# A two-layer graph network: when GpSimd waits for PE before it gathers, and what is prepared first

## What is computed

```python
def _L0_gnn_ref(hn, src, dst):
    sums = jax.ops.segment_sum(hn[src], dst, num_segments=N_NODES)
    deg = jax.ops.segment_sum(jnp.ones((dst.shape[0],)), dst, num_segments=N_NODES)
    return jnp.where(deg[:, None] > 0, sums / jnp.maximum(deg[:, None], 1.0), 0.0)

def _L1_gnn_ref(features, abs_distances, rel_vec, edge_index, w1, b1, w2, b2):
    R = jax.nn.relu(abs_distances[:, None] @ w1 + b1) @ w2 + b2      # 384 radial weights per edge
    Y = spherical_harmonics(rel_vec)                                 # of rel_vec / |rel_vec|
    ...
            acc = acc + _NORM[i] * jnp.einsum('euv,ef,evi,ofi->euo', Rb[..., k], Yf, Fb, C)
    ...
    return out.at[dst].add(msg)

x = _layernorm(x + _L0_gnn_ref(x, src, dst), axis=-1)
x = _layernorm(x + _L1_gnn_ref(x, edge_weight, edge_attr_3, edge_index, ...), axis=-1)
```

## Time and profile before

| | us |
|---|---|
| median of 3 runs | 5155.01 |
| lowest and highest run | 5135.04 and 5165.75 |
| the profiled execution | 5126.5 |
| its span in the trace | 5124.8 |
| mean granted clock of PE in it | 0.879 |

### The profile page before, as it was taken

The page is one execution under the profiler, slowest core; times in us unless marked ns, Lnnn a source line. Parts: engine busy times, 40 slices in busy tenths (PEclk is TensorE's granted clock), DMA queues, the critical chain, the costliest instruction groups (busy, mean ns, idle before and its releaser), DMA issues. The chain is left out here.

```text
span 5124.8 us, 49999 instructions
## 1 busy us (share of the span) xinstructions
PE 3895.7 (76%) x15196; PEld 1997.9 (39%) x15196; DVE 3493.9 (68%) x4460; ACT 685.1 (13%) x1038; POOL 2969.8 (58%) x3001
## 2 busy tenths in 40 slices
PE   3777777777777777874388888888888888888862
PEld 1334343333333333332244444444444444444432
DVE  7655565555655555554478787878878888887864
ACT  0110101010101010100011111111111111111110
POOL 3555454555454545455566666666666666666645
PEclk9888888888888888886599999999999999999985
DMA  2101010010100101000122222222222222222211
GB/s 62 31 22 27 19 30 21 19 27 22 29 19 21 28 21 27 21 20 19 28 48 51 47 47 47 54 47 48 47 47 50 52 47 47 49 52 47 47 33 20
DMA packets 168166, 184.47 MB, mean 36 GB/s; under 512 B 57123, under 2 KB 135238, under 8 KB 161608
## 3 DMA queue, kind: packets, MB, share of 16 engines
q1 hardware_dynamic: 72486, 134.98, 9.3%
q0 software_dynamic: 95648, 49.16, 6.6%
HBM read 121.30 MB, written 62.61 MB: 36 GB/s over the span
## 5 line engine op out<-in xcount | busy, mean ns | idle before, releaser
L566 POOL DMA_INDIRECT got<-x_d,idx x1568 | 1601.8, 1022 | 818.4 <-issue 467.8
L834 PE MATMUL ps_r<-wc,hid 128*128 128x384 f32 x3136 | 1215.1, 529 | 378.4 <-DVE prod L1409 327.9
L834 PEld LDWEIGHTS ps_r<-wc,hid 128*128 128x128 f32 x3136 | 623.2, 205 | 981.5 <-DVE prod L1409 440.4
L762 PE MATMUL ps_r<-rest_f,hid 128*128 128x448 bf16 x1715 | 689.1, 402 | 216.0 <-DVE prod L1136 136.1
L1401 DVE TENSOR_TENSOR prod<-ps_r,f_along 128x768 f32<-128x768 f32 (+1 forms) x588 | 507.6, 863 | 425.2 <-PE ps_r L834 213.0
L762 PE MATMUL ps_r<-inv_len,hid 128*128 128x448 bf16 x1715 | 687.1, 401 | 63.9 <-issue 63.7
L762 PE MATMUL ps_r<-w_sb,hid 128*128 128x448 bf16 x1715 | 684.2, 399 | 64.9 <-issue 64.9
L1136 DVE TENSOR_TENSOR prod<-ps_r,hot_l 128x448 f32<-128x448 f32 x245 | 146.9, 618 | 617.9 <-remote 459.8
L519 POOL DMA_INDIRECT got<-in_x_dram,idx_deep x350 | 341.8, 976 | 377.4 <-PE ps_r L762 262.1
L519 POOL DMA_INDIRECT f_across<-in_x_dram,idx_deep x350 | 331.1, 946 | 312.1 <-PE ps_r L762 210.3
L519 POOL DMA_INDIRECT f_along<-in_x_dram,idx_deep x350 | 332.3, 949 | 309.1 <-PE ps_r L762 194.9
(11 more groups left out here) (189 smaller groups left out, 4755.9 us busy)
## 6 DMA issues: line engine op xcount, KB each, us to landing
run_d<-runs_t SPq DMA_DIRECT2D x196, 256.0 KB
hid<-weight_t SPq DMA_DIRECT2D x98, 512.0 KB
got<-x_d,idx POOLq DMA_INDIRECT x1568
frame_d<-x_sb SPq DMA_DIRECT2D x7, 1008.0 KB
frame<-frame_d SPq DMA_DIRECT2D x98, 72.0 KB
frame_b<-frame_d SPq DMA_DIRECT2D x98, 72.0 KB
got<-in_x_dram,idx_deep POOLq DMA_INDIRECT x350
f_along<-in_x_dram,idx_deep POOLq DMA_INDIRECT x350
```

What stands on the lines that cost most here:

```text
L566: pool.indirect_dma_start(got[k][:, t, :], None, x1_d, bass.IndirectOffsetOnAxis(ap=idx[k][:, t:t + 1], axis=0)).then_inc(got2_landed[k], 16)
L762: mm = pe.matmul(found[g % 3], hot_s[k][:, g, a, :], part[:, a * LN * D:(a + 1) * LN * D], start=(a == 0 and n == 0), stop=(a == BL - 1 an ...
L834: mm = pe.matmul(ps_r[:, g % 2, t, 0:RD], hid[k][:, col:col + P], wc[:, :], start=True, stop=True)
```

## The change

Three things are changed.

1. GpSimd in layer 0. PE posts a new semaphore, `found_steps`, after each of the first six of the seven node blocks of a found tile (six posts per tile, 42 per pair, 2058 in all). GpSimd waits on it before every gather, and against the block that lies five before (`AHEAD`): the 13 gathers of an even block are spread over the 24 steps of an odd one, the 12 of an odd block over the 18 of an even one. The first five blocks (63 gathers) carry no such wait.
2. GpSimd in layer 1. `radial_ready` is posted per tile (16 per block instead of 6), GpSimd waits before every gather, for tile T(b-1) + `BEYOND[t]`. SP, DVE and the last wait of GpSimd count in the new unit. The wait for `idx_ready` moves, with threshold b-1.
3. Preparation. SP loads dst, src, x, edge_weight, then edge_attr. GpSimd pads edge_attr and w2. DVE copies the first indices before the flag. The cast of x to its high bf16 part goes from DVE to ACT, between its fourth and fifth copy of turned weights. Squares, sums, roots, reciprocals and scaling of edge_attr go into `make_frames`, per span. `wc` is made after the first pair of layer 0.

```diff
+BEYOND = (-4, -3, -1, 0, 1, 3, 4, 5, 5, 6, 6, 8, 8, 9, 11, 11)
-WAITS_AT = (0, 4, 8)
+AHEAD = 5
...
-            sp.wait_ge(pads_set, 7)
+            sp.wait_ge(pads_set, 4)
+            load_nodes_or_edges(sp, x_sb[:, :, :].rearrange("p j f -> p (j f)"),
+                                x.rearrange("n f -> (n f)"), NPP * D, loaded_x)
+            sp.wait_ge(pads_set, 5)
+            load_nodes_or_edges(sp, w_sb, edge_weight, COLS, loaded_w)
+            sp.wait_ge(other_pads_set, 2)
             load_nodes_or_edges(sp, unit[:, :, :].rearrange("p t c -> p (t c)"),
                                 edge_attr.rearrange("e c -> (e c)"), 3 * COLS, loaded_attr)
-            load_nodes_or_edges(sp, w_sb, edge_weight, COLS, loaded_w)
-            load_nodes_or_edges(sp, x_sb[:, :, :].rearrange("p j f -> p (j f)"),
-                                x.rearrange("n f -> (n f)"), NPP * D, loaded_x)
...
-                        sp.wait_ge(radial_ready, GROUPS * (b - 1))
+                        sp.wait_ge(radial_ready, T * (b - 1))
...
+            pool.wait_ge(consts_made, 6)
+            pool.memset(unit[96:P, E_REST:COLS, :], 1.0).then_inc(other_pads_set, 1)
+            pool.wait_ge(other_pads_set, 1)
+            pool.memset(w2_sb[H:P, :], 0.0).then_inc(other_pads_set, 1)
...
-                    pool.wait_ge(idx_deep_ready, 2 * i + q + 1)
+                    if not first:
+                        pool.wait_ge(idx_deep_ready, 2 * (i - 1) + q + 1)
                     for k in range(DEEP):
                         if not (first and q == 0):
                             pool.wait_ge(terms1_ready, DEEP * (2 * i + q - 1) + k + 1)
                             pool.wait_ge(got1_landed[k], 16 * (FETCHED_PAIR * i + q * FETCHED[k % 2]))
                         pool.sem_inc(pool_go, 1)
                         pair, odd = DEEP * i + (DEEP * q + k) // 2, (DEEP * q + k) % 2
-                        found_earlier = FOUND_PAIR * pair - (0 if odd else FOUND[1])
+                        found_earlier = FOUND_PAIR * (pair - AHEAD // 2) - (0 if odd else FOUND[1])
                         for t in range(FETCHED[odd]):
-                            if t in WAITS_AT and not (first and q == 0 and k == 0):
-                                pool.wait_ge(found_ready, found_earlier + WAITS_AT.index(t) + 1)
+                            if not (first and DEEP * q + k < AHEAD):
+                                pool.wait_ge(found_steps, (BL - 1) * found_earlier
+                                             + (t + 1) * (BL - 1) * FOUND[1 - odd] // FETCHED[odd])
                                 pool.sem_inc(pool_go, 1)
...
-                    pool.wait_ge(idx_ready, b + 1)
                     if rounds > 0:
+                        pool.wait_ge(idx_ready, b - 1)
                         pool.wait_ge(rotated_in, b - 1)
                         pool.wait_ge(f0_copied, b - 1)
                     pool.sem_inc(pool_go, 1)
                     for t in range(T):
-                        if rounds > 0 and t in (2, 10):
-                            pool.wait_ge(radial_ready, GROUPS * (b - 1) + 2 * (t // 10))
+                        if rounds > 0:
+                            pool.wait_ge(radial_ready, T * (b - 1) + BEYOND[t])
                             pool.sem_inc(pool_go, 1)
...
+                if c == 4:
+                    act.wait_ge(loaded_x, 48)
+                    act.wait_ge(dst_split, 1)
+                    act.copy(hi, x_blocks).then_inc(parts_ready, 1)
...
+                    if j == (2 if first else 0):
+                        if first:
+                            turn0(1, 1, 0)
+                        act.wait_ge(lensq_ready, i + 1)
+                        act.activation(small[:, 0, :], small[:, 0, :], ACT.Sqrt).then_inc(len_ready, 1)
...
+                        if a < BL - 1:
+                            mm.then_inc(found_steps, 1)
...
-                    mm = pe.matmul(ps_r[:, g % 2, t, 0:RD], hid[k][:, col:col + P], wc[:, :], start=True, stop=True)
-                mm.then_inc(radial_ready, 1)
+                    pe.matmul(ps_r[:, g % 2, t, 0:RD], hid[k][:, col:col + P], wc[:, :], start=True, stop=True
+                              ).then_inc(radial_ready, 1)
...
+            def first_indices(done):
+                for q in range(2):
+                    done(dve.tensor_copy(idx_deep[q][:, :], src_all[:, q * DEEP * T:(q + 1) * DEEP * T]))
+                for k in range(2):
+                    done(dve.tensor_copy(idx[k][:, :], src_all[:, k * T:(k + 1) * T]))
+                done(dve.tensor_copy(src_all[:, COLS:COLS + 2 * DEEP * T], src_all[:, 0:2 * DEEP * T]))
...
-            step = COLS // 4
-            for c in range(4):
-                u = unit[:, c * step:(c + 1) * step, :]
-                v = sq[:, 0:3 * step].rearrange("p (t c) -> p t c", c=3)
-                s.settle()
-                s.mark(dve.tensor_tensor(v, u, u, ALU.mult))
-                s.settle()
-                ins = dve.tensor_reduce(inv_len[:, c * step:(c + 1) * step], v, AX.X, ALU.add)
...
-            s.mark(dve.reciprocal(inv_len[:, :], inv_len[:, :]))
-            s.mark(dve.tensor_tensor(unit[:, :, :], unit[:, :, :], spread(inv_len[:, :], 2, 3), ALU.mult))
...
-                dve.tensor_copy(hi, x_blocks).then_inc(parts_ready, 1)
...
+                length, squares = small[:, 0, :], f[:, :, 0, :]
+                s.mark(dve.tensor_tensor(squares, cut, cut, ALU.mult))
+                s.settle()
+                dve.tensor_reduce(length, squares, AX.X, ALU.add).then_inc(lensq_ready, 1)
+                dve.wait_ge(len_ready, n + 1)
+                s.mark(dve.reciprocal(length, length))
+                s.settle()
+                s.mark(dve.tensor_tensor(cut, cut, spread(length, 2, 3), ALU.mult))
...
             layer0(0, True)
+            make_wc()
+            dve.wait_ge(loaded_attr, 48)
             make_frames(0)
```

More of the change, by code:

```diff
@@ L218, in build_program @@
         ps_m = ctx.enter_context(nc.psum_tensor("ps_m", [P, 2, 512], F32))
+        x_blocks = x_sb[:, :, :].rearrange("p (a l) f -> p a f l", l=LN)
+        hi, mid, lo, left = (room.rearrange("p (a f l) -> p a f l", a=BL, f=D) for room in parts + [span_room])
         iota = ps_r[:, 1, 1, 0:P]
@@ L617, in layer0 @@
                     take_terms(16 * (FETCHED_PAIR * i + (FETCHED_PAIR if q else FETCHED[k])), j % DEEP, k)
-                    if first and j == 0:
-                        act.wait_ge(lensq_ready, 1)
-                        act.activation(inv_len[:, :], inv_len[:, :], ACT.Sqrt).then_inc(len_ready, 1)
-                    else:
+                    if not (first and j in (0, 2)):
                         turn0(b - 1, 1 - k, DEEP * i + (j - 1) // 2)
@@ L1083, in _ @@
-            ins.then_inc(lensq_ready, 1)
-            dve.wait_ge(loaded_net, 64)
-            blocks = w2_sb[:, 0:3 * MUL * MUL].rearrange("h (q u v) -> h q u v", q=3, u=MUL)
-            vec = w2_sb[:, 3 * MUL * MUL:RD].rearrange("h (u v m) -> h u v m", u=MUL, m=3)
-            scalars, axis, across = (wc[:, 128 * n:128 * (n + 1)].rearrange("h (v u) -> h u v", u=MUL) for n in range(3))
-            a0 = wtmp[:, :].rearrange("h (u v) -> h u v", u=MUL)
-            s.mark(dve.tensor_scalar(a0, vec[:, :, :, 0], C_A0, None, ALU.mult))
@@ L1091, in _ @@
-            s.mark(dve.tensor_scalar(scalars[:, :, 0:MUL], blocks[:, 0], C_SS, None, ALU.mult))
-            s.mark(dve.tensor_scalar(scalars[:, :, MUL:2 * MUL], blocks[:, 1], C_SV, None, ALU.mult))
-            s.mark(dve.tensor_scalar(axis[:, :, 0:MUL], blocks[:, 2], C_VS, None, ALU.mult))
-            s.mark(dve.tensor_scalar(across[:, :, MUL:2 * MUL], vec[:, :, :, 1], -C_A1, None, ALU.mult))
-            s.settle()
-            s.mark(dve.scalar_tensor_tensor(axis[:, :, MUL:2 * MUL], vec[:, :, :, 2],
-                                            C_A2 * 2.0 / 3.0, a0, ALU.mult, ALU.add))
@@ L1106, in split_x @@
             def split_x():
-                x_blocks = x_sb[:, :, :].rearrange("p (a l) f -> p a f l", l=LN)
-                hi, mid, lo, left = (room.rearrange("p (a f l) -> p a f l", a=BL, f=D) for room in parts + [span_room])
                 dve.wait_ge(loaded_x, 48)
-                dve.wait_ge(w_copied, (COLS + P - 1) // P)
-                dve.tensor_copy(hi, x_blocks).then_inc(parts_ready, 1)
                 dve.wait_ge(parts_ready, 1)
```

55 lines of the change are left out of this document (35 added, 20 removed).

## The result

| | us |
|---|---|
| median before, 4 runs beside the changed kernel | 5145.02 |
| median after, 4 runs | 4744.68 (4716.86 to 4757.47) |
| ratio | 0.9226, 95% interval 0.915 to 0.930 |
| profiled execution before, after | 5126.5, 4742.59 |

What follows compares the result with a forecast made beforehand. No engine is always busy; the scans per block set the pace, with PE stalled by gather trains. Terms -290 - 50 + 0 + 17 = -323 from 5126.5 give 4803.5, with the median 28.5 above: 4832 us, range 4480 to 5130.

Steps and rivals of the forecast that it cites:

- The mechanism: Both layers: long unbroken trains of GpSimd gathers hold PE's sequencer and messages; a train's first gathers cost nothing.
- Rival A: PE's stalls sit at fixed places of its own loop, from instruction supply; pacing does nothing; 5139 us, chance 0.13.
- Part 1: Layer 0's waits before each gather: 3.0 us per block saved, -290 us; bounds 0 and -640.
- Part 4: Frames made per span in DVE's chain: 4.9 us each, seven times 34, half hidden; +17 us, bounds 0 and +34.
- half of each of two stalls: Layer 0, per pair of blocks: pacing removes half of PE's two stalls, 3.0 us per block.
- DVE's "remote" waits: Sign of being right: DVE's "remote" wait before the selection falls under half of 460 us.
- The lead: Layer 0 gathers wait on the block five back; costs nothing, as ring and indices are seven deep.
- Part 2: Layer 1's waits and posts per radial tile: -0.5 us per block, -50 us; bounds -255 and +100.
- D: Rival: the forecast, but layer 1 gets to its floor, GpSimd's 21.1 us per block; 4627 us, chance 0.12.
- Part 3: Preparation before the first found tile: shorter chain, but first gather train may hold PE; 0 us, bounds -42 and +15.
- The posts: PE's 2058 new layer 0 messages: cost nothing, bounds 0 and 0.05 us each, 0 to +100 us.
- Rival B: Full release: single gathers with gaps never stall PE; layer 0 -640 us, 4482 us in all, chance 0.18.

Runs made afterwards that it cites:

- e4: Kernel before, plus in layer 0 a GpSimd wait before a block's 7th and 13th gather until its earlier ones have landed; median 5056.95 against 5249.94 us.
- e9: Kernel before with a wait on a step before each gather of layer 0, lead of one block, on a chip where PE is held; ratio 0.947.
- e11: Changed kernel with a cap on gathers under way, two in layer 0 and three in layer 1; ratio to before 0.9271.
- e12: Changed kernel with a small awaited GpSimd fill before every second gather of layer 0 and every third of layer 1; ratio to before 0.9237.
- e2: Kernel before with only the new GpSimd waits of layer 0 and their posts, lead of five blocks; ratio 0.9376.
- e3: Kernel before with only layer 1's new waits and posts; ratio 0.9656.
- e5: Kernel before, unchanged, on another chip, where nothing held PE; 4048.78 us, ratio 0.9993.
- e1: Changed kernel with GpSimd's waits in both layers as before, so only the new preparation and frames; ratio to before 1.001.
- e6: Changed kernel, with GpSimd waiting for landed gathers before the 7th and 13th of its first seven blocks, on a chip holding nothing; ratio to before 0.9996.
- e7: Kernel before with a wait on a step before each gather of layer 0, lead of one block, on a chip holding nothing; ratio 1.0004.

## Why the prediction was right, and where not

**The mechanism** held: trains of gathers hold PE, and the new waits loosen that. e4, e9, e11 and e12 show it each in another way. Rival A (fixed places of PE's loop, a matter of the supply of instructions) falls with e12, in which PE runs the changed kernel's program and no late message is left among the sixty longest waits, and with e4, which gains while PE runs its old program.

**Part 1**, -290: the 343 us of layer 0 hold the frames' 34 too (part 4), so the waits gave some 377, 3.9 per block for 3.0; e2 against e3, without frames, gives 384. This is the term that was sized most wrongly. The reasoning, half of each of two stalls, was too simple. The hint that it failed: I had said that DVE's "remote" waits would fall under half of 460 us, and they fell only to 365 (without the first train). They are half as long but more of them; what shrank beside them is PE's crawl (671.2 to 372.4 us) and its time at the lower clock. The bound that I took for full release, 33 us per pair, can be reached and more: 15.75 us per block, 31.5 per pair, is what e5 needs with the kernel before.

**The lead**, cost at nothing: right for the loop as far as e9 and e2, on two chips, can be compared; wrong for the start, where it is the reason for the unpaced first five blocks. The sixth block made the train longer still: its waits are for steps of the first find, which were all posted by 66 us, so the train has 75 gathers and not 63.

**Part 2**, -50: measured -51 from profile to profile. By e3 it was -171 on another chip. The estimate fits the trace that it was made from, and to some degree that is luck: nothing in its reasoning gave half a microsecond rather than one or two, and the loss in layer 1 is not a property of the kernel alone. Its lower bound has a slip: a block of 24.1 less GpSimd's 21.1 is 3.0, not 2.6, so the floor was -294, and D's time some 39 us too high. e5 shows that floor, 21.05.

**Part 3**, 0 (bounds -42 and +15): measured +10.5 at the first scan. Both halves show: the chain is 37 us shorter, and the train of the first blocks holds the third tile's message till 115. e1, e11 and e12, whose first trains are short or thin, have the first scan at 69 to 70 on chips where PE is held.

**Part 4**, +17: 34 to 35. The 4.9 us per span were right, but that half of it hides had no row behind it, and at the seven span starts none of it does: the scans there are 4.4 to 5.9 us further apart in e6 and in e1 than without the frames, and as far apart in the kernel after (25.8 to 27.0 us). The wait for ACT's root, a guess of 1 us, is 0.46 at its first in the trace of the kernel after.

**The posts**, nothing: e7 against e5. The Trainium skill's rule for completion increments ("TensorE: Matmul & The Clock Gate", section "The cost: per-tile semaphore tail") would have made 54 us of the 2058 by an estimate from the page. The page gives it for the tail after a group of tiles; the measurement decides against carrying it over to posts within a running stream of matmuls: 15.74 us per block with 42 posts per pair more, 15.75 without.

**The sum**, -323 against -384 by profile and -400 by medians: part 1 was 87 us short, part 4 17 too cheap and part 3 10 too good; part 2 was met. The two smaller misses hid a part of the first; that the sum came within 61 us is luck to that extent.

**Rival B**, full release: it did not come from the change, but e5 shows that its state exists. No run reached it on a chip where PE is held: each way to free PE (e11, e12) made GpSimd the bound.

What stays open: what inside the chip the gathers and PE share; what decides whether gathers hold PE at all; and why layer 1 with the old waits takes 24.1 us per block in one trace and 25.6 to 26.3 in others. That the hold goes with density was seen at three paces only. A lead of one block with the new preparation, which by e1 and e9 should win the start as well, was not run.

## What to carry to other kernels

When an engine's messages come late and it crawls on "issue", look at what another engine's queue does in the same microseconds, and at when the stall ends: in the loop of the kernel before it mostly ended some 2.3 us after the last gather of a train, and waits added to the other engine were worth 193 us. Tie such a producer to its consumer's steps from the first block on, not after a free start. And time a variant on more than one chip: the changed kernel gained 400 us here, and e6, the same but for breaks in its first seven blocks, gained nothing in another set of runs.

## What the runs showed that was not expected

A dense train of indirect gathers (0.94 us each, 1.25 apart) holds PE in five of the six sets of runs (kernel before 5145 to 5276 us): its messages come late, mostly by some microseconds and once by 46, and it crawls, in the first train at one matmul in 2.8 us. It does nothing in the sixth (4049 us). At 1.56 us per gather, with a pause after every second, no late message is left among the longest waits, with as many gathers in the first train.
